# Second layer begun by quarters of the rows, with attention rows interleaved by four, in a four-layer graph network kernel

## What is computed

```python
h = relu(layernorm(x)); x = x + L0(h)   # softmax(q . (adj @ k)) * v over all nodes
h = relu(layernorm(x)); x = x + L1(h)   # 8-head attention, see below
h = relu(layernorm(x)); x = x + L2(h)   # hypergraph convolution, twice
h = relu(layernorm(x)); x = x + L3(h)   # attention with exp(weight) * adj

def L1(x, adj):                         # HEAD_DIM 32, 8 heads
    q, k, v = x @ Wq.T + bq, x @ Wk.T + bk, x @ Wv.T + bv
    scores = (q_head @ k_head.T) * 32 ** -0.5 * (adj + adj)
    ctx = softmax(scores) @ v_head
    return ctx @ Wo.T + bo
```

## Time and profile before

| | us |
|---|---|
| median of 3 runs | 3081.29 |
| lowest, highest | 3079.47, 3081.74 |
| profiled execution, its own time | 3079.83 |
| its span, first to last instruction | 3078.0 |
| TensorE busy | 2976.1 (97%) |
| VectorE busy | 1893.0 (61%) |
| ScalarE busy | 1473.6 (48%) |
| GpSimd busy | 692.9 (23%) |

### The profile page before, as it was taken

The page is one execution under the profiler, slowest core; times in us unless marked ns, Lnnn a source line. Parts: engine busy times, 40 slices in busy tenths (PEclk is TensorE's granted clock), DMA queues, the critical chain, the costliest instruction groups (busy, mean ns, idle before and its releaser), DMA issues.

```text
span 3078.0 us, 63372 instructions
## 1 busy us (share of the span) xinstructions
PE 2976.1 (97%) x22896; PEld 2353.4 (76%) x22896; DVE 1893.0 (61%) x4170; ACT 1473.6 (48%) x2729; POOL 692.9 (23%) x1241
## 2 busy tenths in 40 slices
PE   7999999999999999999999999999999999999999
PEld 6687786877878777788777887778867788677886
DVE  2698426984269742787437874378643786438863
ACT  1684217833178331783327833277322773238722
POOL 0243002430024300242002420034200342013410
PEclk9999999999999999999999999999999999999999
DMA  4302213022130231302313013121132212221200
GB/s 169 90 2 90 76 70 90 2 90 86 59 90 2 90 108 44 84 3 89 131 30 75 19 73 131 39 66 45 58 119 53 52 59 66 97 67 38 80 8 14
DMA packets 98905, 204.35 MB, mean 66 GB/s; under 512 B 11024, under 2 KB 42128, under 8 KB 98576
## 3 DMA queue, kind: packets, MB, share of 16 engines
q1 hardware_dynamic: 98576, 199.96, 20.9%
HBM read 136.75 MB, written 8.65 MB: 47 GB/s over the span
## 4 chain that ended last, share of the span: by engine, by line
PE 68%; issue 11%; DVE 8%; SPq 5%; POOL 4%; ACT 3%; DMA 1%; DVEq 0%; POOLq 0%; ACTq 0%
PE ps L1077 37%; PE ps L1300 11%; PE ps L1224 7%; SPq L446 4%; PE ps L1372 4%; PE ps L1252 4%; PE ps L1202 3%; POOL H L557 3%; DVE Z L787 2%; DVE stats L608 1%; DVE h L845 1%; PE ps L1114 1%; POOL nm L545 1%; ACT Z L1002 1%; DMA qS<-qlo 1%
## 5 line engine op out<-in xcount | busy, mean ns | idle before, releaser
L787 DVE CUSTOM_DVE_ANT_0 Z<-ps,adjN 128x1024 f32<-128x1024 f32 x512 | 623.8, 1218 | 69.9 <-PE ps L1202 69.9
L1002 ACT ACTIVATE Z<-Z,nm 128x1024 f32<-128x1024 f32 x512 | 587.1, 1147 | 66.7 <-POOL nm L545 66.7
L1224 PE MATMUL ps<-ident,Z 128*128 128x128 f32 x4096 | 547.8, 277 | 26.5 <-ACT Z L1002 17.6
L1224 PEld LDWEIGHTS ps<-ident,Z 128*128 128x128 f32 x4096 | 459.7, 141 | 139.3 <-issue 64.1
L1202 PE MATMUL ps<-kS,qS 128*128 128x512 f32 x1024 | 372.1, 446 | 28.4 <-DMA qS<-qlo 28.4
L534 POOL TENSOR_SCALAR ve<-mv 128x4 f32<-128x4 f32 x80 | 15.7, 196 | 1340.1 <-DVE mv L613 1339.4
L557 POOL TENSOR_SCALAR H<-adjN 128x128 fp32r<-128x128 f32 (+1 forms) x456 | 316.8, 695 | 0.0
L545 POOL TENSOR_TENSOR nm<-nm,minus 128x1 f32<-128x1 f32 x512 | 97.1, 190 | 767.4 <-DVE nm L787 762.8
L1077 PE MATMUL ps<-mh,adjT 128*128 128x256 f32 x1024 | 223.6, 379 | 0.0
L1077 PE MATMUL ps<-v,P 128*128 128x257 f32 x1024 | 223.6, 379 | 0.0
L1077 PE MATMUL ps<-hT,t3T 128*128 128x512 f32 x512 | 221.0, 592 | 0.0
(11 more groups left out here) (170 smaller groups left out, 5673.5 us busy)
## 6 DMA issues: line engine op xcount, KB each, us to landing
adjT<-adjT_in SPq DMA_DIRECT2D x8, 4096.0 KB, 13.1
adjN<-adj_in SPq DMA_DIRECT2D x8, 4096.0 KB, 17.3
adjT<-adjT_in SPq DMA_DIRECT2D x8, 2048.0 KB, 9.1
qS<-qhi SPq DMA_DIRECT2D x112, 128.0 KB, 2.5
qS<-qlo SPq DMA_DIRECT2D x112, 128.0 KB, 2.5
kS<-khi SPq DMA_DIRECT2D x96, 128.0 KB, 2.4
kS<-klo SPq DMA_DIRECT2D x96, 128.0 KB, 2.5
adjT<-adjT_in SPq DMA_DIRECT2D x8, 1536.0 KB, 12.0
```

Of the source, the lines that this page charges most:

```text
L787: dve.tensor_tensor_reduce(Z[:, u % ZS], ps[:, 2 * (u % 2):2 * (u % 2) + 2].rearrange("p a n -> p (a n)"), adjN[:, u // HEADS], SCORE_SCAL ...
L1002: act.activation(Z[:, u % ZS], Z[:, u % ZS], ACT.Exp, bias=nm[:, u:u + 1], accum_out=sm[:, u:u + 1]).then_inc(exps.sem, 1)
L1224: mm = pe.transpose(ps[:, turn_bank((u, s)), rows(a)], Z[:, u % ZS, rows(NT // 2 * s + a)], ident[:])
```

## The change

- The features of Wq, Wk and their biases are permuted on the host so that the four heads of a group are interleaved: partition p belongs to head p mod 4. `stack` then reads partitions j, j+4, ... and writes partitions r, r+4, ...; `pick` is built to match.
- L0's residuals, statistics, GpSimd's two steps, the shift, the normalisation and the transposes go by quarters, two tiles at a time (`norm_scale_quarters`, `shift_quarter`, `normalise_quarter`, `transpose_quarter`). ScalarE, not VectorE, copies the transposed quarter to `hT1`, one instruction of 512 columns.
- The six first products are built from quarter products of 256 columns (`project_quarter`). The order of `KQ` puts both keys of the first half first, then both queries of the first half, then both keys of the second half. The first two use banks 6 and 7, whose reader is long done.
- Three of the four dummy matmuls are gone.
- `LASTS` is in a new order, and the first scores wait for the fifth copy (before: the third).
- SyncE queues `qS` for j = 0 before the second half's keys, and the two halves of `kS` for j = 2 are one copy of twice the size.

The core of the diff (changed signal counts and a few renumbered waits are left out):

```diff
     ORDER = HEAD_ORDER
-    KQ = ((0, 0, 0), (0, 0, 1), (0, 1, 0), (1, 0, 0), (1, 0, 1), (0, 1, 1), (1, 1, 0), (1, 1, 1))
-    KQ_BANK = (0, 1, 2, 3, 0, 1, 6, 7)
+    KQ = ((0, 0, 0), (0, 0, 1), (0, 1, 0), (0, 1, 1), (1, 0, 0), (1, 0, 1), (1, 1, 0), (1, 1, 1))
+    KQ_BANK = (6, 7, 0, 1, 2, 3, 6, 7)
+    QUARTERS = NT // 2
+    QUARTER = 2 * P
     KQ_FIRST = 6
-    LASTS = ((0, 0, 0, 4, 4), (0, 0, 1, 5, 4), (1, 0, 0, 3, 4), (0, 1, 0, 6, 5), (0, 1, 1, 7, 5), (1, 1, 0, 4, 6))
+    LASTS = ((0, 0, 0, 4, 1), (1, 0, 0, 5, 3), (0, 1, 0, 6, 4), (1, 1, 0, 7, 4), (0, 0, 1, 4, 5), (0, 1, 1, 5, 6))
     SCORE_SCALE = 2.0 * float(HD) ** -0.5
     W_SCALE = 1.0 / float(D) ** 0.5
...
-                        to = dst[HD * r:HD * r + HD].rearrange("p (g j) n -> p g j n", j=HPG)[:, :, j, cols]
-                        sp.dma_start(to.bitcast(F32), src[HD * j:HD * j + HD, :, cols].bitcast(F32)).then_inc(done.sem, 16)
+                        to = dst[r:P:HPG].rearrange("p (g j) n -> p g j n", j=HPG)[:, :, j, cols]
+                        sp.dma_start(to.bitcast(F32), src[j:P:HPG, :, cols].bitcast(F32)).then_inc(done.sem, 16)
...
-                sp.wait_ge(*lo_s(b, 5))
+                sp.wait_ge(*lo_s(b, 4))
+                stand(sp, waited_sp)
+                stack_q(0, 0)
+                sp.wait_ge(*lo_s(b, 6))
                 stand(sp, waited_sp)
                 stack_k(1, 0)
-                sp.wait_ge(*lo_s(b, 6))
-                stand(sp, waited_sp)
-                stack_q(0, 0)
+                stack_q(0, 1)
                 stack_k(1, 1)
-                stack_q(0, 1)
-                stack_k(0, 2)
-                stack_k(1, 2)
+                stack(kS, (khi, khi, klo, klo), HPG - 2, slice(0, N), kS_in[0][HPG - 2])
...
+            def norm_scale_quarters(b):
+                for q in range(QUARTERS):
+                    of = slice(2 * q, 2 * q + 2)
+                    pool.wait_ge(*mvs(b, NT + 2 * q + 2))
+                    stand(pool, waited_pool)
+                    pool.tensor_scalar(ve[:, of], mv[:, of, 1], EPS, 1.0, ALU.add, ALU.mult).then_inc(ves.sem, 1)
+                    pool.wait_ge(*ves(b, after_quarter(q)))
+                    pool.tensor_tensor(rstd[:, of], ve[:, of], mhalf[:, of], ALU.pow).then_inc(rstds.sem, 1)
...
-                residual0(0)
-                for s in range(NH):
-                    for t in range(TPH * s, TPH * (s + 1)):
-                        if t + 1 < NT and t != TPH:
-                            residual0(t + 1)
-                        statistics1(t)
-                        if t % TPH:
-                            aggregate(b, 1, t - 1)
-                    aggregate(b, 1, TPH * (s + 1) - 1)
-                    if s == 0:
-                        residual0(TPH + 1)
-                        shift(b, 1, 0)
-                hT_copies(b, 1, 0)
-                shift(b, 1, 1)
+                def shift_quarter(q):
+                    of = slice(2 * q, 2 * q + 2)
+                    dve.wait_ge(*rstds(b, after_quarter(q)))
+                    dve.scalar_tensor_tensor(nmr[:, of], mv[:, of, 0], -1.0, rstd[:, of], ALU.mult, ALU.mult).then_inc(nmrs.sem, 1)
+                for q in range(QUARTERS):
+                    residual0(2 * q)
+                    residual0(2 * q + 1)
+                    statistics1(2 * q)
+                    statistics1(2 * q + 1)
+                    if q:
+                        shift_quarter(q - 1)
+                    aggregate(b, 1, 2 * q)
+                    aggregate(b, 1, 2 * q + 1)
+                shift_quarter(QUARTERS - 1)
                 def lower_kq(n):
                     s, w, g = KQ[n]
...
+                def normalise_quarter(q):
+                    act.wait_ge(*nmrs(b, after_quarter(q)))
+                    for t in (2 * q, 2 * q + 1):
+                        act.activation(h[:, t, 0:D], x[:, t], ACT.Relu, bias=nmr[:, t:t + 1],
+                                       scale=rstd[:, t:t + 1]).then_inc(hs.sem, 1)
+                def hT_quarter(q):
+                    act.wait_ge(*hT_ps(b, 2 * DT + q + 1))
+                    act.activation(hT1[:, :, QUARTER * q:QUARTER * (q + 1)],
+                                   ps[:, 4 + q % 2].rearrange("p (c n) -> p c n", c=DT), ACT.Copy).then_inc(hTs.sem, 1)
+                normalise_quarter(0)
+                hT_quarter(0)
+                normalise_quarter(1)
+                hT_quarter(1)
+                normalise_quarter(2)
+                upper_kq(0)
+                upper_kq(1)
+                normalise_quarter(3)
+                hT_quarter(2)
+                hT_quarter(3)
+                for n in range(2, KQ_FIRST):
...
-                keep_warm(6, 3)
...
-                transpose_h(b, 1, 0)
-                keep_warm(6, 1)
-                pe.wait_ge(*hTs(b, 3 * DT))
-                pe.wait_ge(*x0s(b, NT))
+                def transpose_quarter(q):
+                    if q >= 2:
+                        pe.wait_ge(*hTs(b, 2 * DT + q - 1))
+                    for c in range(DT):
+                        for a in range(2):
+                            t = 2 * q + a
+                            pe.wait_ge(*hs(b, NT + t + 1))
+                            mm = pe.transpose(ps[:, 4 + q % 2, QUARTER * c + P * a:QUARTER * c + P * (a + 1)], h[:, t, rows(c)], ident[:])
+                    mm.then_inc(hT_ps.sem, 1)
+                def project_quarter(n, q):
+                    s, w, g = KQ[n]
+                    part = q % 2
+                    cols = slice(QUARTER * q, QUARTER * (q + 1))
+                    mm = product(ps[:, KQ_BANK[n], QUARTER * part:QUARTER * (part + 1)],
+                                 [((Wk1, Wq1)[w][:, c, rows(g)], hT1[:, c, cols]) for c in range(DT)])
+                    if part == 1:
+                        mm.then_inc(kq_ps.sem, 1)
+                transpose_quarter(0)
+                keep_warm(7, 1)
                 pe.wait_ge(*w1_in(b, 48))
-                for n in range(KQ_FIRST):
-                    if n == GROUPS:
-                        transpose_h(b, 1, 1)
-                    if KQ[n][0] == 1:
-                        pe.wait_ge(*hTs(b, 4 * DT))
-                    if n >= 4:
-                        pe.wait_ge(*lo_s(b, n - 3))
-                    project_kq(n)
+                pe.wait_ge(*hTs(b, 2 * DT + 1))
+                project_quarter(0, 0)
+                transpose_quarter(1)
+                project_quarter(1, 0)
+                pe.wait_ge(*hTs(b, 2 * DT + 2))
+                project_quarter(0, 1)
+                project_quarter(1, 1)
+                transpose_quarter(2)
+                for n in (2, 3):
+                    pe.wait_ge(*x0s(b, 2 * KQ_BANK[n] + 2))
+                    project_quarter(n, 0)
+                transpose_quarter(3)
+                project_quarter(2, 1)
+                project_quarter(3, 1)
+                for q in (2, 3):
+                    pe.wait_ge(*hTs(b, 2 * DT + q + 1))
+                    for n in (4, 5):
+                        if q == 2:
+                            pe.wait_ge(*x0s(b, 2 * KQ_BANK[n] + 2))
+                        project_quarter(n, q)
                 pe.wait_ge(picks.sem, 16)
                 for n, (w, g, s, at, split) in enumerate(LASTS):
                     pe.wait_ge(*lo_s(b, split))
-                    if n == len(LASTS) - 1:
-                        pe.wait_ge(*lasts(b, 1))
+                    if n >= 4:
+                        pe.wait_ge(*lasts(b, n - 3))
                     hi, lo = ((khi, klo), (qhi, qlo))[w]
                     product(ps[:, at], [(pick[:, 2 * w], hi[:, g, half(s)]), (pick[:, 2 * w + 1], lo[:, g, half(s)])]).then_inc(last_ps.sem, 1)
...
-                pe.wait_ge(*lasts(b, 3))
+                pe.wait_ge(*lasts(b, 5))
                 scores(0)
-                pe.wait_ge(*lasts(b, 4))
                 project_kq(KQ_FIRST)
```

More of the change, by code:

```diff
@@ L202, in build_program @@
         x_free = signal("x_free", 1)
-        kS_in = [[signal(f"kS_in{s}{j}", 64) for j in range(HPG - 1)] for s in range(NH)]
+        kS_in = [[signal(f"kS_in{s}{j}", 64) for j in range(HPG - 1 - s)] for s in range(NH)]
         qS_in = [[signal(f"qS_in{s}{j}", 64) for j in range(HPG - 1 + s)] for s in range(NH)]
@@ L215, in build_program @@
         mvs = signal("mvs", 5 * NT)
-        ves = signal("ves", 5 * NH)
-        rstds = signal("rstds", 5 * NH)
-        nmrs = signal("nmrs", 5 * NH)
+        ves = signal("ves", 5 * NH + 2)
+        rstds = signal("rstds", 5 * NH + 2)
+        nmrs = signal("nmrs", 5 * NH + 2)
         hs = signal("hs", 3 * NT)
-        hT_ps = signal("hT_ps", 3 * 2 * DT)
-        hTs = signal("hTs", 3 * 2 * DT)
+        hT_ps = signal("hT_ps", 2 * 2 * DT + QUARTERS)
+        hTs = signal("hTs", 2 * 2 * DT + QUARTERS)
         adjT_in_s = signal("adjT_in_s", 16)
@@ L378, in after, with after_quarter, after_tiles @@
         def after(l, s):
-            return NH * l + s + 1
+            return NH * l + s + 1 + (2 if l > 1 else 0)
```

(35 more changed lines are left out.)

19 lines of the change are left out of this document (8 added, 11 removed).

## The result

The changed kernel takes 3013.8 us (median of 4 runs, 3012.42 to 3014.79) against 3080.85 beside it: a ratio of 0.9782, with a 95% interval of 0.9765 to 0.9799. Forecast were 3023 and a range of 3010 to 3050. The profiled execution's span went from 3078.0 to 3012.2 us, 65.8 less.

The account below looks back on a forecast made before the run. TensorE was taken as nearly always busy or fed, so only its stands, non-result work and slow clock count. 8 x 2.5 + 28.4 + 10 = 58.4 us off 3079.83 gives 3021.4, 3023 for the median; range 3010 to 3050.

Parts of the forecast that it names:

- the opening: Layer 2's start: quartering the chain to the first product starts the first scores 2.5 us earlier in each of 8 batches.
- the clock: Score loop after the 2.24 us stand: the slow clock would no longer occur, saving 10 us in the run.
- The DMA waits: TensorE's waits for stacked copies at the fifth and seventh heads: both go, 28.4 us in the run.
- Its size and count are equal: Stacked copies with rows four apart: taken to issue at 0.60 us, like consecutive rows.
- I take the count: Merged j = 2 copy: an issue costs by count, so qS for the seventh head lands at 486.9, before TensorE's 488.4.
- an issue by bytes: Merged j = 2 copy, other end: qS for the seventh head lands at 489.4, costing 1.0 us per batch.
- The margin: Fifth head's copy: lands at 481.7, wanted at 482.75, 1.0 us to spare, 0.3 if the one long issue falls there.
- Rival (a): Clock falls anyway, at the new opening or the PTa wait: 3042 us, chance 0.14.
- Without the 2.24 us stand I expect none: Seventh head: no slow clock once that stand is gone; 5 x 1.1 + 2 x 2.2 = 10 us.
- They filled a wait, so alone they are worth nothing: Layer 2's hand-over: removing three dummies (2.6 us) gains nothing by itself.
- (b): ScalarE's longer list delays key uppers, scores start as before, one DMA wait of 1.0 stays: 3051 us, chance 0.10.
- (c): Copies with rows four apart are dear; at 1.3 us an issue the seventh head comes 6.0 us later: 3129, chance 0.07.

Follow-up runs that it names:

- quarters_alone: Changed kernel with heads in consecutive blocks, j = 2 copies unmerged and the old queue order, quarters kept: 3051.48 us, ratio 0.991 to the kernel before.
- block_rows: Changed kernel with heads back in blocks of 32 consecutive partitions, quarters and queue order kept: 3048.48 us, ratio 0.9899 to the kernel before.
- before_interleaved: Kernel before the change with rows interleaved by four and nothing else: 3076.42 us beside 3078.45, ratio 0.9993.
- late_split_picks: Changed kernel, eighth key-query product's rounding moved later, picks reordered so first scores wait for ScalarE's third copy: 3007.92 us.
- before_filled: Kernel before the change with two dummy float32 matmuls in TensorE's 2.24 us stand ahead of the seventh scores: 3066.3 us, ratio 0.9958.
- no_dummy: Changed kernel without its last dummy product: 3012.47 us beside 3013.8.
- before_both: Kernel before the change with interleaved rows and the merged j = 2 copy, no quarters, old queue order: 3047.9 us, ratio 0.9893.
- before: The kernel before the change, unedited: 3080.85 us beside the changed kernel.
- before_merged: Kernel before the change with the two kS halves for j = 2 in one 256 KB copy: 3084.35 us, ratio 1.0015.

## Why the prediction was right, and where it was not

**The number.** 3023 was forecast and 3013.8 measured, 9 us less. 5.7 us of them are the opening (25.7 for 20), 2.1 the clock; 0.4 goes the other way, the DMA wait that was left. The last 1.8 lie between the profiled execution and the median: the forecast added 1.5, and the changed kernel's median is 0.25 below its profiled execution.

**The opening.** Right in mechanism. The term was 2.5 us and measured 3.2. The chain to the first quarter product was reckoned at 6.2 us and is 5.9; the stretch from there to the picks at 12.0 and is 11.7; the picks and ScalarE's copies to the first scores at 3.55 and are 3.56. So half of the error lies in the first part and half in the second. TensorE leaves the value products 4.6 us after the first residual, as forecast. From there to the first quarter product 1.6 us were reckoned and 1.3 are measured (449.64 to 450.94), hand-overs counted a little long; in the second part twelve transposes were taken at 1.6 us and are three times 0.43 (the last four start at 457.18, the products behind them at 457.61). The power step was taken at its upper end, 1.01, and is 0.69, but that is not where the time came from: the two tiles of h were ready 0.15 us before TensorE left the value products. For the same reason the range's low end was reasoned wrongly: "the two-column power at 0.2 gives up to 0.8 a batch more, 3010". That gain could not have come, as TensorE had no idle time there to give back. The measured 3.2 is near the upper bound that was given for TensorE alone (3.3). `quarters_alone`, whose first scores also come 21.2 us after the first residual in every batch, bears the term out.

**The DMA waits.** The sum, 28.4 us, was right (28.0), in part by luck. The reason for it was wrong in one step: "Its size and count are equal; the nearest rows are 0.60 us an issue. I take that" and "By it the sum stays as it is, the waits being gone either way". The waits are not gone either way: `block_rows` has them back, at 34.7 us. The interleaving was treated as neutral, and the merged copy as cheap by its own nature ("I take the count"). They are one thing: the 256 KB copy costs its count only when its rows lie four apart. The sum held because the change has both edits, not because each does what the working said. The end that was priced, an issue by bytes, 1.0 us a batch, was right about the issue: the last copy of the seventh head leaves 2.5 us later in `block_rows`, as reckoned. It was too cheap because the copy was then taken to land after 2.6 us as before, while it is 3.45 from its issue to the scores, and because the slow clock comes back with the wait.

The Trainium skill as cited there (SBUF — State Buffer, "Door 1: the DMA port swizzle": 32 consecutive rows reach 8 of 16 ports) was the better guide than the use made of it. The runs agree in direction; that the ports are the reason is not shown, as no run tried another spacing or counted ports. The same 199.96 MB of the queue took 20.9% of the engines' time before and, in the row of the queue in the profile (packets, MB, share), after:

```profile
q1 hardware_dynamic: 96016, 199.96, 18.3%
```

The rows do this, not the merged copies: in `before_interleaved`, which changes nothing but the rows, the share is 17.8%, and the packets of 2 KB took 84 ns at the median over its trace, where they took 146 before. The window of the earlier trace rows at 200 GB/s was the warning: the engines were busy 0.87 of the time at one 128 KB copy per issue, so twice the bytes an issue could not go at the same pace.

**The margin.** The fifth head's copy was forecast to land 1.0 us before it is wanted, 0.3 with the one long issue. It has no margin: in the changed kernel one issue near 459.4 takes about 1.3 us more than the others (2.62 for two) where 0.7 was allowed, the first scores come 0.6 us sooner than forecast, and 0.36 us of wait is left in one batch. `late_split_picks` shows the same edge.

**The clock.** Right in mechanism and place; `before_filled` isolates it. The size was 10 and is 12. Rival (a), a fall at the new opening, did not come, also not in `no_dummy`, where TensorE stands 0.69 us in place of the last dummy. Whether transposes count for the clock no run here shows. The step "Without the 2.24 us stand I expect none" held in the changed kernel, but a stand does not always bring the fall: the first batch before and the profiled `quarters_alone` had stands of 1.8 to 2.1 us at the seventh head and kept 1.00.

**The dummies.** "They filled a wait, so alone they are worth nothing" holds for the old order; in the new one they would cost 18.8 us, against 21 reckoned.

**Rivals (b) and (c).** The scores do wait for ScalarE's copies (0.42 us; the forecast had 0.8, from 473.0 to 473.8), but from 3.2 us earlier, not from the old time. Issues with rows four apart start 0.64 us apart as before, apart from the long one that both kernels have.

**What adds up.** `before_both` gives 32 us and `quarters_alone` 28; together 60 of the 67. The rest was not isolated. What both leave is the wait at the fifth head, 10.0 us in `before_both` and 0.4 in the changed kernel, and the new order of the queue, with the queries of j = 0 first, is the part of the change that stands in neither; no run has it alone.

## What to carry to other kernels

Where a chain over several engines opens a stage, cut its first piece, not its work: two tiles instead of four brought the first product 4 us forward at equal matmul time, and the dummies that had hidden the chain then had to go. Before merging DMAs to save issues, ask whether the bytes go by as fast; here merging paid only with the rows spread. A stand ahead of dense matmuls costs more than its length when the clock falls in it, and can be priced by filling it with work that is thrown away.

## What the runs showed of the hardware

- Copies from SBUF to SBUF of 32 partitions: four apart, a 128 KB copy lands after 2.1 us and 256 KB after 2.4 to 2.5; consecutive, 2.4 to 2.7 and 3.5 to 4.9 (medians of `before`, `before_merged`, `block_rows`). SyncE issues either at one per 0.64 us until the transfers fall behind; then the issue itself takes up to 1.4 us.
- About once in each batch an issue takes 0.2 to 1.4 us more than its neighbours, before and after, at a place that moves with the kernel. Its cause stays open.
- GpSimd's power takes 1.01 us on 128 x 4 and 0.69 on 128 x 2.
- The clock fell after the stands of 0.9 to 1.7 and 2.1 to 2.3 us in seven of eight batches of the kernel before, and not in the profiled execution of `quarters_alone`, with stands of 1.6 to 1.9 and 1.8 to 2.1 in the same places; two dummies of 1.99 us in the second stand kept it at 1.00 in `before_filled`. What tells the cases apart was not tested.
